# Self-attention in a decoder layer: probabilities turned by DMA, three f16 products for the mixing, values projected by tiles of 128 tokens

## The reference

```
x = x + attn(layernorm(x))          # self-attention, 16 heads of 128, this change
x = x + xattn(layernorm(x), ctx)    # cross-attention, 16 heads of 32, causal mask
x = x + ffn(layernorm(x))           # SwiGLU with 8 LoRA experts, top 2

def attn(x):                        # B=32, S=100, E=512, H=16, D=128
    q, k, v = x@wq, x@wk, x@wv
    qn = rms_norm(q, q_scale); kn = rms_norm(k, k_scale)
    p  = softmax(einsum('bqhd,bkhd->bhqk', qn, kn))
    return einsum('bqhd,hde->bqe', einsum('bhqk,bkhd->bqhd', p, v), wo)
```

## Time and profile before

| | us |
|---|---|
| median of 3 runs | 2805.93 (2804.98 to 2810.42) |
| the profiled execution | 2802.11 |
| its span, first to last instruction | 2800.3 |
| PE busy in the span | 2644.0 |
| DVE busy | 1679.3 |
| ACT busy | 1193.4 |
| POOL busy | 707.3 |
| DMA queue, share of 16 engines | 25.1% |

### The profile page before, as it was taken

The page is one execution under the profiler, slowest core; times in us unless marked ns, Lnnn a source line. Parts: engine busy times, 40 slices in busy tenths (PEclk is TensorE's granted clock), DMA queues, the critical chain, the costliest instruction groups (busy, mean ns, idle before and its releaser), DMA issues.

```text
span 2800.3 us, 46316 instructions
## 1 busy us (share of the span) xinstructions
PE 2644.0 (94%) x16726; PEld 1504.9 (54%) x16726; DVE 1679.3 (60%) x3701; ACT 1193.4 (43%) x2390; POOL 707.3 (25%) x672
## 2 busy tenths in 40 slices
PE   7999999999999999999987999998999999999988
PEld 4555555555555555555545446445445455455467
DVE  7776655655555555666657566566565565565554
ACT  4444444444444444444433542543543443443524
POOL 2222211211112111121212332422432422422413
PEclk9999999999999999999997999999999999999999
DMA  5444343444434344455421000000001001000000
GB/s 149 122 116 107 94 95 95 110 96 94 107 82 113 90 100 111 102 124 128 107 88 60 1 16 21 16 15 26 10 16 34 2 16 35 1 16 23 1 17 11
DMA packets 320477, 179.69 MB, mean 64 GB/s; under 512 B 266984, under 2 KB 269672, under 8 KB 320232
## 3 DMA queue, kind: packets, MB, share of 16 engines
q1 hardware_dynamic: 320232, 176.47, 25.1%
HBM read 78.66 MB, written 32.77 MB: 40 GB/s over the span
## 4 chain that ended last, share of the span: by engine, by line
PE 80%; DVE 12%; issue 4%; POOL 2%; ACT 2%; DMA 0%; DVEq 0%; SPq 0%; POOLq 0%; ACTq 0%
PE ps L1280 21%; PE ps L1281 20%; PE ps L1282 20%; PE ps L1356 3%; DVE mem L1114 2%; PE ps L1424 2%; POOL mem L589 2%; PE ps L1425 2%; PE ps L1426 2%; DVE mem L1118 2%; DVE mem L928 1%; PE ps L1332 1%; DVE mem L990 1%; PE ps L1434 1%; PE ps L1438 1%
## 5 line engine op out<-in xcount | busy, mean ns | idle before, releaser
L1280 PE MATMUL ps<-mem 128*128 128x512 f16 (+6 forms) x3524 | 1183.6, 344 | 37.1 <-DVE mem L990 24.1
L1281 PE MATMUL ps<-mem 128*128 128x512 f16 (+6 forms) x3524 | 1180.1, 343 | 0.0
L1282 PE MATMUL ps<-mem 128*128 128x512 f16 (+6 forms) x3524 | 1169.5, 342 | 0.0
L1280 PEld LDWEIGHTS ps<-mem 128*128 128x128 f16 (+2 forms) x3524 | 382.9, 109 | 353.6 <-issue 35.6
L1282 PEld LDWEIGHTS ps<-mem 128*128 128x128 f16 (+2 forms) x3524 | 382.0, 108 | 309.1 <-issue 5.3
L1281 PEld LDWEIGHTS ps<-mem 128*128 128x128 f16 (+2 forms) x3524 | 383.9, 109 | 290.0 <-issue 5.9
L589 POOL TENSOR_TENSOR mem<-mem 128x8 f32<-128x8 f32 x100 | 163.6, 1636 | 937.6 <-DVE mem L930 937.6
L632 POOL TENSOR_TENSOR mem<-mem 128x500 f32<-128x500 f32 (+1 forms) x231 | 268.1, 1161 | 360.3 <-ACT mem L862 207.9
L1236 DVE TENSOR_TENSOR mem<-mem 128x500 f16<-128x500 f32 (+1 forms) x231 | 144.6, 648 | 188.1 <-ACT mem L844 184.1
L990 DVE SCALAR_TENSOR_TENSOR mem<-ps,mem 128x512 f32<-128x512 f32 x100 | 69.1, 691 | 303.0 <-PE ps L1282 303.0
L646 POOL TENSOR_TENSOR mem<-mem 100x400 f32<-100x400 f32 x128 | 108.2, 856 | 332.7 <-DVE mem L1128 332.7
(11 more groups left out here) (123 smaller groups left out, 3436.1 us busy)
## 6 DMA issues: line engine op xcount, KB each, us to landing
x<-mem SPq DMA_DIRECT2D x100, 256.0 KB, 2.1
mem<-x SPq DMA_DIRECT2D x75, 256.0 KB, 2.8
mem<-in_x SPq DMA_DIRECT2D x50, 256.0 KB, 3.3
mem<-x SPq DMA_DIRECT2D x12, 1000.0 KB
out<-mem SPq DMA_DIRECT2D x6, 1000.0 KB
mem<-in_wq SPq DMA_DIRECT2D x4, 1024.0 KB, 6.3
mem<-in_wk SPq DMA_DIRECT2D x4, 1024.0 KB, 6.4
mem<-in_wv SPq DMA_DIRECT2D x4, 1024.0 KB, 5.4
```

What stands on the lines that cost most here:

```text
L1280: pe.matmul(out_ap, ah, bh, start=(i == 0), stop=False)
L1281: pe.matmul(out_ap, ah, bl, start=False, stop=False)
L1282: mm = pe.matmul(out_ap, al, bh, start=False, stop=(i == len(pairs) - 1))
```

## The change

It alters only the self-attention and where the weight pieces of the second part are split.

- Probabilities: one buffer instead of two. The inverse sum is scaled by 1024 (a further small DVE instruction), ACT writes the f16 high half into `p_split`, POOL the low half, and SP turns both with one DMA transpose of 112 rows and 1024 columns into `pT` (two slots). The four transposes on PE and `take_pT` go. `p_split` is filled with zeros once, on POOL.
- Mixing: `three` per head, so 12 f16 matmuls with 128 stationary columns and 100 moving ones, one step later than before (`mix_values(n-1)`); the halves of oT are scaled back by 1/1024.
- Values: projected per tile of 128 tokens at the step before their first use, into a PSUM bank of their own, split by ACT and DVE into `vt`; `place_values` on SP moves runs of rows to the sequences in `v` (three slots) with SBUF to SBUF DMAs, 56 of them a group.
- The output projection comes one step later and has its own bank; the ring of `oT` shrinks to 512 columns; squares of q and k are made and summed one after the other in a buffer of half the size.
- Two weight pieces fewer are split inside the attention (13), with one staging slot, loaded one step ahead instead of two; the other seven go beside the first cross-attention, up to two per sequence.

The diff, cut to what the text speaks of:

```diff
-ORING = 640
+P_SCALE = 1024.0
+ROWS = 112
+ORING = 512
...
+def valued_at(n):
+
+    return [u for u in range(NHG * TILES) if first_use(u) - 1 == n]
+
...
-            if hg * 32 + (t * P + P - 1) // S + 1 == n]
+            if hg * 32 + (t * P + P - 1) // S + 2 == n]
...
-        pT = cut([HG, S])
+        probs = cut([HG, S])
...
+        pT = cut([2, 2 * HG, ROWS], F16)
+        p_split = cut([2, 2, HG, D], F16)
...
         oT_hi = cut([HG, ORING], F16)
         oT_lo = cut([HG, ORING], F16)
-        v = cut([2, HG * D])
+        vt = cut([2, 2, HG * D], F16)
+        v = cut([3, 2, HG * D], F16)
...
-        ps_vw, ps_s, ps_pT, ps_o = (ps[:, b, :] for b in range(4, 8))
+        ps_v, ps_s, ps_w, ps_o = (ps[:, b, :] for b in range(4, 8))
...
+        def value_runs(u):
+
+            hg, t = divmod(u, TILES)
+            runs = []
+            for b in range(t * P // S, (t * P + P - 1) // S + 1):
+                a, e = max(b * S, t * P), min(b * S + S, t * P + P)
+                runs.append((hg * NB + b, a - t * P, a - b * S, e - a))
+            return runs
...
-        B_SPLIT = [98, 100, 102, 104, 106, 108, 110, 112, 114, 116, 118, 124, 125, 126, 127]
-        B_ROWS, B_STATS, B_NORM = 110, 119, 121
+        B_SPLIT = [98, 100, 102, 104, 106, 108, 110, 112, 114, 116, 118, 124, 126]
+        B_ROWS, B_STATS, B_NORM = 111, 120, 122
+
+        def slot_b(n):
+
+            return 1 if n < len(B_SPLIT) else n % 2
...
-            return [k for k, at in enumerate(B_SPLIT) if at - 2 == n]
+            return [k for k, at in enumerate(B_SPLIT) if at - 1 == n]
...
-            return range(len(B_PIECES))[B_IN_A + b:B_IN_A + b + 1]
+            return range(len(B_PIECES))[B_IN_A + 2 * b:B_IN_A + 2 * b + 2]
...
-                if n >= 2:
-                    sp.wait_ge(c["wlo"], n - 1)
-                sp.dma_start(stage_b[:, n % 2, 0:chunks * width].rearrange(
-                    "p (c n) -> p c n", c=chunks), src).then_inc(c[f"wld{n % 2}"], 16)
+                if before_b(n) >= 0:
+                    sp.wait_ge(c["wlo"], before_b(n) + 1)
+                sp.dma_start(stage_b[:, slot_b(n), 0:chunks * width].rearrange(
+                    "p (c n) -> p c n", c=chunks), src).then_inc(c[f"wld{slot_b(n)}"], 16)
...
+            def place_values(u):
+
+                sp.wait_ge(s["vlo"], u + 1)
+                if u >= 2:
+                    sp.wait_ge(s[f"vb{u % 2}"], placed(u - 2))
+                for n, row, to, count in value_runs(u):
+                    if n >= 3:
+                        sp.wait_ge(s["o"], n - 2)
+                    sp.dma_start(v[to:to + count, n % 3, :, :], vt[row:row + count, u % 2, :, :]
+                                 ).then_inc(s[f"vb{u % 2}"], 16)
+
+            def turn_probs(n):
+
+                sp.wait_ge(s["plo"], n + 1)
+                if n >= 2:
+                    sp.wait_ge(s["o"], n - 1)
+                sp.dma_start_transpose(pT[:, n % 2, :, :],
+                                       p_split[0:ROWS, n % 2, :, :, :].rearrange("p a h k -> p (a h k)")
+                                       ).then_inc(s[f"pT{n % 2}"], 16)
...
+            for n in range(FIRST_STEP, STEPS + 3):
+                for u in valued_at(n - 1):
+                    place_values(u)
                 for w in summed_at(n - 1):
                     store_sum(w)
                     if w + 2 < ALL:
@@ -529,9 +586,10 @@
                         sp.wait_ge(s[f"st{w % 3}"], stored(w))
                     load_rows(yn, rows_of(x1, 0, GB), GB, "yn_in")
                     load_keys(keys_of(0, GB), GB)
+                if 0 <= n + 1 < STEPS:
+                    turn_probs(n + 1)
                 for u in projected_at(n - 1):
                     turn_tile(u)
-            store_sum(ALL - 1)
...
-                pool.tensor_tensor(probs[0:S, n % 2, :, :], probs[0:S, n % 2, :, :],
+                pool.tensor_tensor(probs[0:S, :, :], probs[0:S, :, :],
                                    rden[0:S, :].unsqueeze(2).to_broadcast([S, HG, S]),
                                    ALU.mult).then_inc(s["norm"], 1)
+
+            def probs_lo(n):
+                pool.wait_ge(s["phi"], n + 1)
+                pool.tensor_tensor(p_split[0:S, n % 2, 1, :, 0:S], probs[0:S, :, :],
+                                   p_split[0:S, n % 2, 0, :, 0:S], ALU.subtract).then_inc(s["plo"], 1)
...
+            pool.memset(p_split[:, :, :, :, :], 0.0).then_inc(s["pz"], 1)
...
+                    probs_lo(n + 1)
...
-                act.wait_ge(s["qp"], u + 1)
-                if u:
-                    act.wait_ge(s["ss"], u)
-                act.activation(sq[:, 0:HG, :], bank("q", u).rearrange("p (h d) -> p h d", d=D),
-                               ACT.Square).then_inc(s["sqq"], 1)
-                act.wait_ge(s["kp"], u + 1)
-                act.activation(sq[:, HG:2 * HG, :], bank("k", u).rearrange("p (h d) -> p h d", d=D),
-                               ACT.Square).then_inc(s["sqk"], 1)
+                for m, kind in enumerate(("q", "k")):
+                    act.wait_ge(s[kind + "p"], u + 1)
+                    if u or m:
+                        act.wait_ge(s["ss"], 2 * u + m)
+                    act.activation(sq[:, :, :], bank(kind, u).rearrange("p (h d) -> p h d", d=D),
+                                   ACT.Square).then_inc(s["sq" + kind], 1)
...
-            def take_v(n):
-                act.wait_ge(s["vp"], n + 1)
+            def probs_hi(n):
+                act.wait_ge(s["norm"], n + 1)
+                if n == 0:
+                    act.wait_ge(s["pz"], 1)
                 if n >= 2:
-                    act.wait_ge(s["o"], n - 1)
-                act.activation(v[0:S, n % 2, :], ps_vw[0:S, :], ACT.Copy,
+                    act.wait_ge(s[f"pT{n % 2}"], 16 * (n // 2))
+                act.activation(p_split[0:S, n % 2, 0, :, 0:S], probs[0:S, :, :],
+                               ACT.Copy).then_inc(s["phi"], 1)
+
+            def take_v(u):
+                act.wait_ge(s["vp"], u + 1)
+                if u >= 2:
+                    act.wait_ge(s[f"vb{u % 2}"], placed(u - 2))
+                act.activation(vt[:, u % 2, 0, :], ps_v[:, :], ACT.Copy,
                                scale=V_SCALE / (X_SCALE * W_SCALE)).then_inc(s["ve"], 1)
-
-            def take_pT(n):
-                act.wait_ge(s["pTp"], n + 1)
-                if n:
-                    act.wait_ge(s["o"], n)
-                act.activation(pT[0:S, :, :], ps_pT[0:S, 0:HG * S].rearrange(
-                    "p (h t) -> p h t", h=HG), ACT.Copy).then_inc(s["pTe"], 1)
...
-            for n in range(FIRST_STEP, STEPS):
-                if n >= 0:
-                    take_pT(n)
+            for n in range(FIRST_STEP, STEPS + 1):
+                if 0 <= n - 1 < STEPS:
+                    take_o_hi(n - 1)
                 if 0 <= n + 1 < STEPS:
                     exponentials(n + 1)
-                    take_v(n + 1)
+                for u in valued_at(n):
+                    take_v(u)
                 for u in turned_tile(n):
                     rows_hi(u)
-                if n >= 0:
-                    take_o_hi(n)
                 for u in projected_at(n - 1):
                     split_qk(u)
+                if 0 <= n + 1 < STEPS:
+                    probs_hi(n + 1)
...
+            def sum_squares(u, m):
+
+                i = u % 2
+                dve.wait_ge(s["sq" + "qk"[m]], u + 1)
+                dve.tensor_reduce(ss[:, i, m * HG:(m + 1) * HG], sq[:, :, :], AX.X,
+                                  ALU.add).then_inc(s["ss"], 1)
...
-                if n >= 2:
-                    dve.wait_ge(s["pTp"], n - 1)
+                if n:
+                    dve.wait_ge(s["plo"], n)
...
+                dve.wait_ge(s["den"], 2 * n + 1)
+                dve.tensor_scalar(den[0:S, :], den[0:S, :], 1 / P_SCALE, None,
+                                  ALU.mult).then_inc(s["den"], 1)
+                dve.wait_ge(s["den"], 2 * n + 2)
                 dve.reciprocal(rden[0:S, :], den[0:S, :]).then_inc(s["rden"], 1)
...
-                    op = dve.tensor_tensor(oT_lo[:, :, at:at + count],
-                                           ps_o[:, 0:HG * S].rearrange("p (h t) -> p h t", h=HG)
-                                           [:, :, col:col + count],
-                                           oT_hi[:, :, at:at + count], ALU.subtract)
+                    op = dve.scalar_tensor_tensor(
+                        out=oT_lo[:, :, at:at + count],
+                        in0=ps_o[:, 0:HG * S].rearrange("p (h t) -> p h t", h=HG)[:, :, col:col + count],
+                        scalar=1 / P_SCALE, in1=oT_hi[:, :, at:at + count], op0=ALU.mult,
+                        op1=ALU.subtract)
                 op.then_inc(s["olo"], 1)
+
+            def take_v_lo(u):
+                dve.wait_ge(s["ve"], u + 1)
+                dve.scalar_tensor_tensor(out=vt[:, u % 2, 1, :], in0=ps_v[:, :],
```

(77 more changed lines are left out.)

51 lines of the change are left out of this document (26 added, 25 removed).

## The result

The changed kernel takes 2700.14 us (median of four runs, 2697.87 to 2703.52) against 2805.45 us for the kernel before on the same chip (2802.31 to 2810.42): a ratio of 0.9625, 95% interval [0.9614, 0.9637]. That is 105 us saved. The forecast was 2648, so two thirds of the expected 158 us came. The profiled executions give the same: 2802.11 us before, 2698.37 us after.

A forecast was written before the change was run, and what follows sets the result against it. TensorE's columns were taken as the bound, busy for 2644 of 2800.3 us. From 2802.1, 208 us off PE, 44 of new waits and 7 for tail and weight pieces gave 2645, median about 2648; range 2605 to 2725.

The forecast's parts named there:

- Work of PE: Self-attention on TensorE: fewer value matmuls 73 us, transposes gone 61, mixing 40, two waits gone 34; ideal step 9.2 us.
- Latency of the transposes: Self-attention: qk tiles land late for scores in the shortest step pairs; 12 us for tiles turned twice, 12 for timing error.
- short pairs: Self-attention: a step without qk beside one without v or wo, 15.2 us, 24 in all, 1 us to spare.
- the chain: Self-attention: counted from a step's scores, pT issued at 8.6 us and the qk tile at 9.7, landing at 14.
- DVE's scaling of q in the first quarter: Self-attention, first quarter: scaling q frees the bank that k's projection takes, 7.2 against 7.3 us; 10 us of new waits.
- Values copied by DMA: Self-attention: 224 runs of value rows copied by DMA, 0.37 us of SP each, 0.65 us a step.
- rival B: Self-attention: tiles and values land late at most steps, 1 us in each of 128; 2732 us, chance 0.18.
- Rival D: Self-attention: PE's gaps grow until the granted clock falls and the gain is eaten; about 2806 us, chance 0.03.
- Load: Self-attention: DMA engines take 6.4 of 9.2 us a step, 70%, upper bound 86%; no bound on average, but queueing.
- Tail and what follows: Behind the last row-maximum: 14.3 us to the first transpose, 2 us lost; weight pieces beside cross attention, 5 us.
- A: Self-attention: no new waits, pairs wide enough or the queue shorter than reckoned; 2608 us, chance 0.16.
- C: Self-attention: with one buffer of probabilities the subtraction waits for plo, 11.5 us a step; 2890 us, chance 0.07.

The follow-up runs named there:

- both: Kernel after, with a tile's first two value copies issued in the step that makes it and the qk transpose ahead of the probabilities': 2642.99 us, 0.9421.
- oneturn: Kernel after, without the repeated transpose of tiles needed in a fifth slot (slot holds zeros, output not the layer's): 2665.78 us, ratio 0.9502.
- early: Kernel after, with the first two value copies of a tile issued in the step that makes it, the third where it was: 2659.11 us, 0.9484.
- nocopy: Kernel after, without the 224 value copies and the waits on them, v filled once with a constant: 2649.61 us, ratio 0.9441.
- unread copies: Kernel after, with value copies made but not waited for, the mixing reading weights in place of v: 2664.77 us, ratio 0.9497.

## Why the prediction was right and wrong

The time was in the range and the direction right; 52 us of the gain were missing, and 2700 lies outside the forecast's own spread of 2620 to 2690.

- **Work of PE**: right. Take the version with both edits: 1246.2 - 40.4 = 1205.8 us from first to last maximum. PE is idle for 31.5 us of it and the low clock takes 10.8; this leaves 1163 us. The prediction had 127 x 9.2 = 1168. Against before the work fell by 1336 - 1165 = 171 us, where the forecast had 170 (208 less the 34 of waits and the 4 behind the last maximum). The transposes are gone. A mixing group runs from 604.04 to 604.57 us, 0.53 us (timeline of PE, kernel after):

```profile
604.04 0.21 PE L1363 MATMUL ps<-mem 100*128 100x100 f16 x1
...
604.53 0.21 PE L1365 MATMUL ps<-mem 100*128 100x100 f16 x1
604.57 0.38 PE L1363 MATMUL ps<-mem 128*128 128x512 f16 x1
```

 12 pairs in 0.53 us are 44 ns a pair, so the mixing gained 128 x (0.87 - 0.53) = 44 us where the forecast had 40. The Trainium skill ("TensorE: Matmul & The Clock Gate", section "Back-to-back issue gap") gives about 81 ns for a sustained pair at N=128. The trace does not agree at its 100 columns; by the page's figure, an estimate, the mixing would have lost some 13 us.
- **Latency of the transposes**: right in kind and size. Forecast 24 us of waits on tiles in the short pairs, 12 of it for tiles that are turned twice; measured 25.3 us, 13 of them, and 10.9 without the second turns (`oneturn`), so 14.4 for these. In the example the chain is right by step too: scores at 427.47, pT issued at 436.29, 8.8 us later (forecast 8.6), the doubled transpose at 437.72, the next scores that need it 1.84 us late (forecast 2).
- **DVE's scaling of q in the first quarter**: forecast 10 us, measured 9.3. The match is partly luck: in `early`, `nocopy` and `both`, where PE waits less for DMAs, this wait is 15 to 17 us. The weight pieces of the last quarter (10 us) don't appear among PE's waits: of weight pieces only L950, the low half of one for the self-attention, ended a wait, of 1.4 us.
- **Values copied by DMA**: the step that failed. The forecast priced the copies as load alone, 0.37 us of SP each, and treated only pT and the tile as things that must land by a time. But the copies of a tile stand in SP's program one iteration behind the one in which the tile is made, so that SP first waits out plo and issues the transposes of the iteration before. That wait of the mixing was 0 us in the sum and measured 34 us in the steps and 4.9 in the tail. The words for it stood in rival B ("copies of values stand behind transposes"), which put it at every step; it hit 26.
- **The clock**: 0 us in the sum, 23 us measured (27.5 less 4.7 before). Rival D had the clock fall for long stretches or not at all. Neither came: in the example PE runs at half speed for 5.7 us behind two gaps of 1.84 and 3.31 us, and at full speed behind that. The two missing terms hang together: issuing the copies early took 26 us of idle time and 11 us of low clock, and gave 41 us in all. Slow work counts as busy, which is also why PE's busy time fell by 144 us and not by 175.
- **Load**: the DMA share was 0.66 to 0.76, forecast 0.70. SP's issue of a copy was 0.77 us instead of 0.37, that of pT 1.26 instead of 0.85; unread copies cost 15 us against no copies: 11 of idle time, 8 of it at the scores, and 5 of low clock.
- **Tail and what follows**: forecast 14.3 us from the last maximum, measured 21.1, 4.9 of it a wait on the last copy; the weight pieces beside the cross attention 6 instead of 5.
- **Rivals**: A (2608) and C (2890) didn't occur; the subtraction waited on plo for 0.3 us in all.

The version with both edits, at 2643, is within 5 us of the forecast, in which copies leave on time. That agreement is partly luck: the forecast had 24 us of waits on tiles and 10 on weight pieces that this version does not have (5.2 us at the scores, none on a weight piece of the second part), and it lacked the 7 us more on the scaling of q and the 11 us of low clock.

## What to carry to other kernels

When work moves from an engine to DMAs, list for each DMA the earliest time its data is ready, the place in the issuing queue's program where it goes out, and the time its reader wants it. SP's queue here went through its DMAs in the order of the program and stood for 413 us before the one that was ready last, so the DMA that is ready first should stand first. Here two moves of lines, with no work added or taken away, gave 57 us, and one on DVE another 9. A gap of some us on a busy PE should be priced with the clock behind it: in `early` 26 us less idle time gave 41 us.

## What the runs showed of the hardware

- Copies between SBUF tensors held SP longer than copies to or from device memory (kernel after, by source line; SP's ns min/median/max per issue), here 773 ns against 0.36 to 0.49 us of the load and store at 430 us; a transpose of 1024 columns held it 1.26 us and landed in 3.2 us, one of 2048 columns 2.16 us and 4.5 us (medians):

```profile
L548 SPq DMA_DIRECT2D mem<-mem x224: 548/773/1315, 52.8 to 1306.3; - x112
L556 SPq DMA_TRANSPOSE mem<-mem x128: 1228/1260/7012, 49.2 to 1308.0; - x128
L537 SPq DMA_TRANSPOSE mem<-mem x124: 1772/2161/6411, 29.6 to 1288.7; - x124
```

- A subtraction on POOL with f16 output (and one f16 input) took 1267 ns, where a multiplication of the same shape all in f32 takes 855 (kernel after, groups; which of the differences costs the time isn't shown):

```profile
L659 POOL TENSOR_TENSOR mem<-mem 100x400 f16<-100x400 f32 x128 | 162.2, 1267 | 187.7 <-ACT mem L799 187.7
L653 POOL TENSOR_TENSOR mem<-mem 100x400 f32<-100x400 f32 x128 | 109.3, 854 | 82.9 <-DVE mem L1049 82.9
```

- Weight loads of 100 partitions by 128 columns took 100 ns, as those of 128 by 128, and not the 127 of 128 by 100: of these three kinds the one with 100 columns is the slow one.
- The granted clock fell to half behind gaps of PE that were each shorter than 5 us, inside stretches in which PE was otherwise busy: up to 152.96 us there is one gap of 2.28 us, and from 154.10 us seven matmuls of 512 columns in a row start 0.43 us apart instead of 0.22 (kernel after).
